# LayerNorm of a fused attention and FFN layer: normalized x by PE transposes, or by a transposed load and a product with the roots

## The reference

```python
xn = layernorm(x)                         # mean and variance over the 256 columns
q = xn @ wq                               # 8 heads of 128
k, v = (xn @ wk_down) @ wk_up, (xn @ wv_down) @ wv_up   # 2 key/value heads, rank 32
y = causal_softmax(q k^T / sqrt(128)) v   # four query heads per key/value head
x1 = x + y @ wo
out = x1 + layernorm(layernorm(x1)) * ln_g + ln_b
```

## Time and profile before

| | us |
|---|---|
| median of 3 runs (461.03 to 465.08) | 462.14 |
| the profiled execution, whole | 460.89 |
| its span on the core | 459.2 |
| first score matmul of window 0 | 41.18 |
| ACT normalizations (128x256), 24 | 0.592 each |
| ACT copies of transposes (128x512), 13 from sh_ps | 0.598 each |

### The profile page before, as it was taken

How to read it: one execution, slowest core, us unless ns; L and a number is a source line. 1 busy time by engine, 2 the same in 40 slices (tenths; PEclk the granted TensorE clock), 3 DMA queues, 4 the chain that set the end, 5 groups by cost and what they waited for, 6 DMA issues and landing times.

```text
span 459.2 us, 6945 instructions
## 1 busy us (share of the span) xinstructions
PE 413.5 (90%) x2556; PEld 244.2 (53%) x2556; DVE 280.7 (61%) x426; ACT 250.5 (55%) x484; POOL 225.1 (49%) x186
## 2 busy tenths in 40 slices
PE   5888889999999999999999999999999998989991
PEld 3573556555655565545655565545656474533541
DVE  6256865656657466556967476553966486614546
ACT  2423337655566665655665665555745656567640
POOL 2002132366635862376635852376336945586352
PEclk9967989999999999999999999999999999999997
DMA  6684900375014601065034601065052601001011
GB/s 207 150 104 124 140 3 1 120 184 79 1 33 55 89 1 47 14 86 77 1 84 52 87 2 47 13 97 66 1 99 35 87 2 47 1 2 47 0 48 46
DMA packets 20609, 27.35 MB, mean 60 GB/s; under 512 B 2528, under 2 KB 12768, under 8 KB 20448
## 3 DMA queue, kind: packets, MB, share of 16 engines
q1 hardware_dynamic: 19712, 25.43, 30.7%
q10 hardware_dynamic: 864, 1.48, 0.9%
HBM read 6.72 MB, written 4.19 MB: 24 GB/s over the span
## 4 chain that ended last, share of the span: by engine, by line
PE 66%; DVE 11%; POOL 7%; ACT 6%; issue 6%; DMA 2%; SPq 0%; DVEq 0%; POOLq 0%; ACTq 0%
PE u_ps L565 13%; PE st_ps L519 12%; PE mx_ps L540 11%; PE sh_ps L576 7%; PE sh_ps L626 6%; PE sh_ps L670 5%; DVE mx_part L966 5%; POOL pr L1288 5%; ACT pr L800 3%; PE mx_ps L546 3%; PE sh_ps L619 2%; DMA qs<-q_lo 2%; POOL pr L1275 1%; PE sh_ps L655 1%; PE sh_ps L611 1%
## 5 line engine op out<-in xcount | busy, mean ns | idle before, releaser
L966 DVE TENSOR_REDUCE mx_part<-mx_ps 128x2 f32<-128x1024 f32 (+3 forms) x160 | 175.4, 1114 | 93.9 <-PE mx_ps L546 55.7
L800 ACT ACTIVATE pr<-st_ps 128x512 f32<-128x512 f32 (+1 forms) x304 | 166.9, 574 | 88.3 <-PE st_ps L519 78.2
L1288 POOL TENSOR_TENSOR pr<-pr 128x768 f32<-128x768 f32 (+4 forms) x60 | 144.4, 2410 | 66.5 <-PE u_ps L565 43.8
L519 PE MATMUL st_ps<-qs,ks 98*128 98x512 f32 (+1 forms) x304 | 140.1, 470 | 10.5 <-ACT pr L800 10.0
L540 PE MATMUL mx_ps<-ks,qs 96*128 96x512 f32 (+3 forms) x384 | 110.6, 369 | 5.3 <-DVE mx_part L966 3.7
L1275 POOL TENSOR_SCALAR_AFFINE_SELECT pr<-pr 128x512 f32<-128x512 f32 x64 | 40.8, 638 | 115.1 <-ACT pr L800 114.9
L519 PEld LDWEIGHTS st_ps<-qs,ks 98*128 98x128 f32 x304 | 56.9, 188 | 63.3 <-ACT pr L800 36.2
L540 PEld LDWEIGHTS mx_ps<-ks,qs 96*128 96x128 f32 x384 | 70.2, 195 | 23.6 <-DVE mx_part L966 9.6
L565 PE MATMUL u_ps<-pr,v 128*32 128x512 f32 (+3 forms) x768 | 72.3, 492 | 1.5 <-POOL pr L1275 1.5
L546 PE MATMUL mx_ps<-mask_r,ident_r 128*128 128x128 f32 (+2 forms) x176 | 46.2, 262 | 0.0
L565 PEld LDWEIGHTS u_ps<-pr,v 128*32 128x32 f32 x768 | 20.1, 109 | 36.9 <-issue 28.6
(11 more groups left out here) (109 smaller groups left out, 329.9 us busy)
## 6 DMA issues: line engine op xcount, KB each, us to landing
qs<-q_hi SPq DMA_DIRECT2D x32, 256.0 KB, 5.6
qs<-q_lo SPq DMA_DIRECT2D x16, 256.0 KB, 6.7
out_y<-y SPq DMA_DIRECT2D x7, 512.0 KB, 3.1
x<-in_x SPq DMA_DIRECT2D x3, 1024.0 KB, 7.9
ks<-k_hi SPq DMA_DIRECT2D x32, 64.0 KB, 5.3
x<-in_x SPq DMA_DIRECT2D x4, 256.0 KB, 5.6
pr<-in_wq ACTq DMA_DIRECT2D x1, 1024.0 KB, 7.6
ks<-k_lo SPq DMA_DIRECT2D x16, 64.0 KB, 5.9
```

Of the source, the lines that this page charges most:

```text
L519: nc.tensor.matmul(st_ps[n % 2][:, 0:nh * width], ks[g][0:KM, kt * P:(kt + 1) * P], qs[g][0:KM, c, h0:h0 + nh, off:CH], start=True, stop=T ...
L800: nc.scalar.activation(pr[:, slot, h0:h0 + nh, off:CH], st_ps[n % 2][:, 0:nh * width].rearrange("p (h q) -> p h q", h=nh), ACT.Exp, scale= ...
L966: nc.vector.tensor_reduce(mx_part[:, t // CT, own, h0:h0 + nh, t % CT], mx_ps[n % 2][:, 0:nh * pitch].rearrange("p (h k) -> p h k", h=nh)[ ...
L1288: last = nc.gpsimd.tensor_tensor(even, even, pr[:, 6 + (e // 2) % 2, h0:h1, off:CH], ALU.add)
```

## The change

x is given a second time, transposed within each batch (xt, done on the host when the input is laid out). SP loads it straight into xnT, one half (512 tokens) at a time. The mean is taken out of the weights instead of x: on PE a matrix of 1/256 gives the column means of wkv (`ck`) and of the two halves of wqk (`cq0`, `cq1`), and the DVE subtracts them (`centre`). The root is spread over the partitions by four transposes of a broadcast column (`rb0`, `rb1`), and the DVE multiplies xnT by it, 128 x 1024 in one instruction per half (`scale_x`). Gone are xn, its normalizations on ACT and on the DVE, the four transpose steps with ACT's copies, and the shift. Each later batch has two steps rb in place of four steps xT, at other places. wq comes in two DMAs. Warm-up matmuls: 6 for 12.

```diff
-WARM = 12
+WARM = 6
-USES_START = ["xT0", "xT1", "k0", "wq0", "qa0", "xT2", "xT3", "k1", "qa1", "wq1", "v", "m0", "qb0", "qb1"]
-WINDOW0 = [["", "xT0"], ["m1", "sum1"], ["sT1", "xT1"], ["rT1", ""], ["f2", "xT2"], ["f3", "m0"],
-           ["sum0", "xT3"], ["sT0", "k0"], ["rT0", ""], ["qa0", ""], ["k1", ""], ["qa1", ""]]
+USES_START = ["ck", "wq0", "rb0", "cq0", "wq1", "k0", "rb1", "qa0", "k1", "qa1", "cq1", "v", "m0", "qb0", "qb1"]
+WINDOW0 = [["", ""], ["m1", "sum1"], ["sT1", "rb0"], ["rT1", "rb1"], ["f2", ""], ["f3", "m0"],
+           ["sum0", ""], ["sT0", "k0"], ["rT0", ""], ["qa0", ""], ["k1", ""], ["qa1", ""]]
...
-WINDOW0_FIRST = [["", ""], ["", "xT0"], ["", "xT1"], ["m1", "wo"], ["", "xT2"], ["sum0", "xT3"],
-                 ["sT0", "m0"], ["rT0", "k0"], ["", "qa0"], ["", "k1"], ["", "qa1"], ["", ""]]
+WINDOW0_FIRST = [["", ""], ["", ""], ["", ""], ["m1", "wo"], ["", ""], ["sum0", "rb0"],
+                 ["sT0", "m0"], ["rT0", "k0"], ["rb1", "qa0"], ["", "k1"], ["", "qa1"], ["", ""]]
...
+            for c in range(NC):
+                for i in range(2 * c, 2 * c + 2):
+                    sp.dma_start(x[:, 0, 2 * i:2 * i + 2, :],
+                                 x_d[0].rearrange("(i t p) d -> i p t d", t=2, p=P)[i]).then_inc(x0_in[i], 16)
+                load_xt(0, c)
...
-            sp.wait_ge(wq_in, 16)
+            sp.wait_ge(wq_in[1], 16)
...
                 put_rows(w, 1, use_no(b, 0, kind, "m1"))
+                if kind == FIRST:
+                    for c in range(NC):
+                        load_xt(1, c)
                 put_rows(w + 1, 0, use_no(b, 0, kind, "m0"))
...
                 stack_lo(("q", 1, 1), ("k", 1, 1))
+                if b + 2 < B:
+                    for c in range(NC):
+                        load_xt(b + 2, c)
...
+                if kind == "ck":
+                    pe.wait_ge(weights_in, 2 * 16)
+                    for d in range(ND):
+                        last = nc.tensor.matmul(bank[:, 0:P], mean_of[:, :], wkv[:, d, :], start=d == 0, stop=d == ND - 1)
+                elif kind == "cq":
+                    wait_start(pe, f"wq{c}")
...
+                elif kind == "rb":
+                    pe.wait_ge(rstd1_ready, c + 1 if nb == 0 else NC + nb)
+                    for t in range(CT):
+                        last = nc.tensor.transpose(bank[:, t * P:(t + 1) * P],
+                                                   rstd1[:, nb, c * CT + t:c * CT + t + 1].to_broadcast([P, P]), ident[:, :])
...
-            def normal(b, t):
...
+            def scale_x(name, n, nb):
...
+                dve.wait_ge(sh_full, start_full(name) if n is None else sh_fills(n))
+                dve.wait_ge(xt_in[c], 16 * (nb + 1))
+                here = xnT[:, :, c * CH:(c + 1) * CH]
+                nc.vector.tensor_tensor(here, bank[:, None, :].to_broadcast([P, ND, CH]), here, ALU.mult).then_inc(done, 1)
...
+            def centre(name, weight):
...
+                dve.wait_ge(sh_full, start_full(name))
+                nc.vector.tensor_tensor(weight, weight, start_bank(name)[:, None, 0:P].to_broadcast([P, ND, P]),
+                                        ALU.subtract).then_inc(start_sem(name), 1)
...
-                dve.wait_ge(rstd1_ready, c + 1)
-                for t in range(c * CT, (c + 1) * CT):
-                    norm1_apply(0, t)
+                if c == 0:
+                    centre("ck", wkv[:, :, :])
+                    scale_x("rb0", None, 0)
+                    centre("cq0", wqk[:, :, 0:P])
```

More of the change, by code:

```diff
@@ L122 @@
     MID: [WINDOW0, WINDOW1],
-    LAST: [without(WINDOW0, "xT0", "xT1", "xT2", "xT3", "k0", "k1", "qa0", "qa1"),
+    LAST: [without(WINDOW0, "rb0", "rb1", "k0", "k1", "qa0", "qa1"),
            without(WINDOW1, "qb0", "qb1", "v", "m0")],
@@ L223, in program @@
         weights_in = sem("weights_in")
-        wq_in = sem("wq_in")
+        wq_in = [sem(f"wq_in{g}") for g in range(NKV)]
         wo_loaded = sem("wo_loaded")
@@ L262, in program @@
         rstd_ready = sem("rstd_ready")
-        xn_ready = sem("xn_ready")
+        xt_in = [sem(f"xt_in{c}") for c in range(NC)]
         x1_ready = sem("x1_ready")
@@ L556, in pv @@
                     if w == 0:
-                        wait_start(pe, "qb1")
+                        wait_start(pe, "qb0")
                 if kt == 0 and not (isinstance(w, int) and w == 0 and c == 0):
@@ L605, in fill @@
                 kind = name.rstrip("0123456789")
[L606 to L612, removed]
+                if kind == "ck":
[4 more added lines that the diff above has]
+                    wait_start(pe, f"wq{c}")
+                    for d in range(ND):
+                        last = nc.tensor.matmul(bank[:, 0:P], mean_of[:, :], wqk[:, d, c * P:(c + 1) * P],
+                                                start=d == 0, stop=d == ND - 1)
+                elif kind == "rb":
[3 more added lines that the diff above has]
+                                                   rstd1[:, nb, c * CT + t:c * CT + t + 1].to_broadcast([P, P]), ident[:, :])
                 elif kind == "k":
                     if n is None:
-                        pe.wait_ge(weights_in, 2 * 16)
-                        wait_start(pe, f"xT{2 * c}")
-                        wait_start(pe, f"xT{2 * c + 1}")
+                        wait_start(pe, "ck")
+                        wait_start(pe, f"rb{c}")
                     for d in range(ND):
@@ L824, in read @@
                                          ).then_inc(wide_ready, 1)
-                if kind in ("sT", "rT", "f"):
+                if kind in ("sT", "rT", "f", "rb", "ck", "cq"):
                     return
                 act.wait_ge(sh_full, start_full(name) if n is None else sh_fills(n))
[L828 to L832, removed]
+                if kind == "k":
                     for gg in range(NKV):
@@ L886, in _ @@
             act.dma_start(upT[:, :, :], up_d).then_inc(weights_in, 16)
-            act.dma_start(wqT, wq_d).then_inc(wq_in, 16)
+            for g in range(NKV):
+                act.dma_start(wqT[:, g * HG:(g + 1) * HG, :], wq_d[:, g * HG:(g + 1) * HG, :]).then_inc(wq_in[g], 16)
             def setup(name, dst, src):
@@ L1001, in stats_of @@
                 norm1_stats(b, range(TT), 2 * NC + b)
[L1003 to L1007, removed]
+            def scale_x(name, n, nb):
+                c = int(name[-1])
+                bank = sh_ps if n is not None else start_bank(name)
+                done = sh_read if n is not None else start_sem(name)
+                dve.wait_ge(sh_full, start_full(name) if n is None else sh_fills(n))
[6 more added lines that the diff above has]
+                                        ALU.subtract).then_inc(start_sem(name), 1)
             def reciprocals(n):
@@ L1364 @@
     up = np.stack([np.asarray(L0_attn_wk_up).T, np.asarray(L0_attn_wv_up).T], axis=1)
-    given = {"x": L0_attn_x, "wq": by_head, "wkv": wkv, "up": up,
+    given = {"x": L0_attn_x, "xt": np.asarray(L0_attn_x).transpose(0, 2, 1), "wq": by_head, "wkv": wkv, "up": up,
              "wo": L0_attn_wo, "ln_g": L0_ffn_ln_g, "ln_b": L0_ffn_ln_b}
```

52 lines of the change are left out of this document (20 added, 32 removed).

## The result

| | before | after |
|---|---|---|
| median, us | 463.01 (461.03 to 465.08) | 469.43 (469.29 to 485.93) |
| the profiled execution | 460.89 | 469.36 |
| its span | 459.2 | 467.6 |
| mean granted clock over the span | 0.975 | 0.964 |

The ratio after to before is 1.0137, interval 1.0077 to 1.0197: slower, by 0.8 to 2.0%. Executions more than 1.5% above the fastest of the same kernel are left out of every ratio here; of the changed kernel's ten in two runs four are so (478 to 486 us), and of e1_warm12's four only the profiled one is left (465.98; the others took 479 to 482).

What follows compares the result with a forecast made beforehand. PE was taken to set the pace from about 60 us. Terms +1.5 +2.1 +2 x 1.1 -1.0 = +4.8, less 1.5, gave +3.3: 464.2 us profiled, 465.4 against the median; range 456.5 to 471.

Steps and rivals of the forecast that it cites:

- the landing of wq: Start: the first half of wq was estimated to land near 7 us, the loads sharing 360 GB/s evenly.
- The step that failed: Start: halving the warm-up matmuls, said to end before any input, was taken at 0, bounds -2 and +3 us.
- the start slips: Rival, start: wq's halves land 2.5 us later and hold up the centring; qa0 near 18, time 468 us; chance 0.10.
- The start's end: First score matmul waits for ACT and DVE to read qb1, moved into a score bank: +1.5 us, bounds +1 and +2.
- The DVE's product: Root steps: the 128x1024 product with one PSUM operand was taken at 1.22 us, ends 1.2 and 2.0.
- Middle batches: Each middle batch: 3.3 us lost to root steps up to m0, 2.2 given back: +1.1, bounds -1.8 and +3.3.
- a period from sums to sums of 103.5 to 104: Sign that the forecast is right: a middle batch's period grows to 103.5 to 104 us from 102.83.
- the rival in which the clock falls in the new waits: Rival, batches: PE's new waits lower its clock, costing 1.7 us in each of three batches: 470.5 us; chance 0.18.
- granted clock under 1.00 after 160 us: Listed among the signs that would show the forecast wrong, for the batches after the start; no size given.
- Batch 0: Batch 0: +1.4 us at sT0, +1.5 at the second root step, 0.8 removed: +2.1, bounds -1 and +3.
- POOL: Windows 1 and 3: PE waits less for POOL's masks, -0.5 us each, -1.0 in all, bounds 0 and -1.5.
- took back 1.5: Three batches: a third of PE's about 4.5 us of waits for ACT was expected to go, -1.5 us.

Runs made afterwards that it cites:

- e1_warm12: The changed kernel with 12 warm-up matmuls again instead of 6, nothing else; 465.98 us in the profiled execution.
- e4: The kernel before with 6 warm-up matmuls instead of 12, nothing else; 465.18 us, ratio 1.0142 to the kernel before.
- x9_before_fill: The kernel before with five more warm-up-form matmuls ahead of the first maxima matmul; 457.91 us profiled, median 459.89, ratio 0.9954.
- x9_again: x9_before_fill run once more, unedited, in five rounds; 461.0 us profiled, median 461.11 beside 462.14, ratio 0.9962 to the kernel before.
- e2: The changed kernel with the start's four banks in another order, so qb1 is not in a score bank; 471.82 us, ratio 1.0346.
- x11: The changed kernel with the batches' scale_x product cut to 2x8 columns a partition, most of xnT left unscaled; 470.3 us.
- e5: The changed kernel with 12 warm-up matmuls, and roots and k0 ahead of the folds of wq; 466.02 us, ratio 1.0121.
- e7: The changed kernel with 12 warm-ups, roots and k0 first, qb1 off the score banks, ACT copying roots, batch root steps moved; 472.39 us profiled, ratio 1.016.
- x10: The changed kernel with 12 warm-ups, the start's banks reordered, and 14 more warm-up-form matmuls ahead of the first maxima; 469.81 us, ratio 1.0189.
- e3: The changed kernel with the middle batches' two root steps at tiles 6 and 8 instead of 2 and 3; 473.94 us profiled, ratio 1.0291.
- e6: The changed kernel, but in the batches ACT copies the roots out of the shared bank and the DVE multiplies from SBUF; 474.45 us, ratio 1.0232.

## Why the prediction was right, and where not

The time, 465.4 forecast against 469.4, lies in the range, and the sign was right, but of the sum less than half was there: +3.3 forecast, +8.4 found. That the range held it is partly luck: its upper end came from rivals for the batches and for the landing of wq, and most of the miss is a term that I had taken at nothing. I also thought a change within 1% the likeliest (0.46); the ratio 1.0137 is over that, though its interval reaches down to 1.0077.

- **The step that failed** is "Half the warm-up matmuls go; they ended before any input. I take 0 here, bounds -2 and +3". It counted what the warm-ups delay and not what they do for the rate of the matmuls behind them. e4 shows it alone: +5.7 to mx. In the changed kernel e1 gives back 3.5 of 5.2. Both are single profiles of a start whose rate differs by up to 2 us between executions (x9_before_fill and x9_again), but all seven starts with six warm-ups agree. I had read the same thing in the earlier trace rows for the wait for q_lo and used it as a rival for the batches only.
- Beside it, the landing of wq was mis-sized: "near 7" by shared bandwidth, and PE waited for it until 8.81, and until 9.28 in e1. In e1 the other 1.7 us of the start are left: mx at 28.05 against 26.39. They are there at qa0 already, 17.04 against 15.30. From the fold to qa0 e1 took 7.8 us, where I had worked out 8.5, so the order on PE was no longer than forecast, and the landing, 2.3 later than near 7, more than covers the rest. It is the landing of the rival *the start slips* (2.5 later, qa0 near 18). No run has an earlier wq, so it is not shown that one would give the 1.7 back.
- **The start's end:** +1.5 forecast, +1.9 found, of it the wait of 1.48 for qb1's q_lo. e2 removed 1.1 of it.
- **The DVE's product:** 1.22 forecast, 1.21 to 1.23 found, at every place. My upper end, the mean of 2.038 in the earlier trace rows, is of single products that took 1.22 to 2.66.
- **Middle batches:** the mechanism and the sizes held. rT1 goes 2.34 behind the roots instead of 1.30 behind xT1, +1.04 (forecast 1.2). Up to f2 it is +2.5 in batch 2 (forecast 2.8). Three removed steps were worth the 2.0 read from the earlier trace rows; the fourth, behind the sums, gave 0.3 in batch 2 (43.92 to 43.60), where I had taken 0.6. Batch 2 is +0.6, as forecast. The sign that I had named for this, a period from sums to sums of 103.5 to 104, did not come: it is 102.92 (187.40 to 290.32), since that period joins the cheaper late half of batch 1 to the dearer early half of batch 2.
- **Batch 1** is +1.3 instead of +0.1: this is the rival in which the clock falls in the new waits, in one batch of three, 1.2 us where it gave 1.7. x11 ties it to the product's wait. The prediction's list of signs has it on the wrong side, rightly: "granted clock under 1.00 after 160 us".
- **Batch 0:** the two waits came as worked out (sT0 waits 1.05, where I had 1.4, and the second roots 1.13, where I had 1.1), yet the stretch is 0.4 shorter. The kernel before lost time to its own falls there: without any (x9_before_fill) it takes 77.6, and the changed kernel, also without any from 45 us on, 79.1. e4_before_warm6, also at 1.00 there, takes 78.1. At equal clock the change so costs 1.0 to 1.5 in batch 0; forecast 1.1.
- **POOL:** PE's wait for its masks went from 1.5 to 0.2, forecast -1.0. PE's wait for ACT fell by 0.8, where I took back 1.5.

What stays open: why the same twelve warm-ups give full rate up to k0 in e1, e5 and e7 and not in x10, and in the kernel before up to mx in two profiles and not in the third (x9_before_fill), and why the fall moves between 45 and 82 us from kernel to kernel. Of the seven starts with twelve, four had half rate somewhere before mx. With six warm-ups all seven profiled starts ran at half rate: the changed kernel twice, e2, e3, e4, e6 and x11. No version here beats the kernel before beyond doubt.

## What to carry to other kernels

Matmuls without input at the start are not idle decoration: before halving them, ask what rate the first real ones run at, and read it from the duration of equal matmuls early and late. A step moved from ACT to the DVE is paid by whoever waits for the shared bank; freeing the bank by a copy helps only if what PE needs next is not behind the same product on the DVE (batch 0 of e6 against its middle batches). When engines' waits move by a microsecond, compare stretches at equal clock before crediting the edit.

## What the runs showed that I had not expected

- The granted-clock column can read 1.00 over matmuls at half rate: e4 from 10 to 21 us, k0 3.75 instead of 1.96.
- The half-rate stretch of batch 0 comes and goes with small edits elsewhere: 64 to 67 us before, none in the changed kernel, 45 to 55 in x9_again, 65 to 82 in e7, part of 45 to 80 in e2, of 45 to 65 in x10, of 60 to 70 in e3 and of 70 to 80 in x11. A gain of 2 to 3 us at the first score matmul so reached the end in one profile of two.
- The stretch from the last v to the end has two lengths, whatever the kernel: 133.6 to 133.7 us in nine profiles, 135.0 to 135.3 in the other five (e3, e4, e6, x9_before_fill, x11). In the five the granted clock falls for some microseconds between 400 and 424 us, where the changed kernel is at 1.00. Two kernels can so differ by 1.5 us at a place that no edit touched.
- A product of 128x1024 from two SBUF operands took 2.56 us beside POOL's sum, 1.22 away from it, and 1.21 beside it with one operand in PSUM.
- Loading wq in two halves brought the first one little: PE could fold at 8.81, with 1.44 us of waiting for it, though it was issued at 1.84. In the eight profiled starts that fold first, that moment lies between 8.81 and 10.03.
